# Router logits of a gated decoder stack: the two parts of the router's weights side by side, and each half's logits in one block ahead of the next units' first products

## The reference

```python
logits = tokens @ router_w.T                 # 1024 tokens x 8 experts
topv, topi = jax.lax.top_k(logits, K)        # K = 2
w = jax.nn.softmax(topv, axis=-1)
gate = jnp.zeros((T, n_experts)).at[jnp.arange(T)[:, None], topi].add(w)
for e in range(n_experts):
    h = jax.nn.gelu(tokens @ w1[e].T, approximate=False)
    out = out + gate[:, e:e + 1] * (h @ w2[e].T)
```

## Time and profile before

| | |
|---|---|
| median of 3 runs | 146.15 us (144.23, 146.15, 146.25) |
| the profiled execution | span 144.6 us from first to last instruction, 1996 instructions; no other time is given for it |
| TensorE, its weight loads | busy 121.0 us (84%), 86.0 us (59%) |
| VectorE | busy 116.2 us (80%) |
| ScalarE, GpSimd | busy 79.8 us (55%), 37.4 us (26%) |
| chain that ended last | TensorE 50%, VectorE 26%, issue 10%, ScalarE 6%, DMA 4% |

### The profile page before, as it was taken

The page is one execution under the profiler, slowest core; times in us unless marked ns, Lnnn a source line. Parts: engine busy times, 40 slices in busy tenths (PEclk is TensorE's granted clock), DMA queues, the critical chain, the costliest instruction groups (busy, mean ns, idle before and its releaser), DMA issues.

```text
span 144.6 us, 1996 instructions
## 1 busy us (share of the span) xinstructions
PE 121.0 (84%) x622; PEld 86.0 (59%) x622; DVE 116.2 (80%) x325; ACT 79.8 (55%) x149; POOL 37.4 (26%) x58
## 2 busy tenths in 40 slices
PE   6999999999999999999999968999999700049890
PEld 4787768486656567876555847777758500035570
DVE  5888985997329999999496986888398899899873
ACT  3343495745565576975453242173438899880540
POOL 1009302310569400396003704422010003000000
PEclk9999999999999999999999977999999995556998
DMA  4996000002079522320000000000000000000004
GB/s 130 300 410 239 0 0 0 0 0 65 24 221 345 159 73 75 97 99 22 5 0 0 0 2 0 0 5 2 0 0 0 0 0 2 0 5 0 0 0 145
DMA packets 4413, 8.76 MB, mean 61 GB/s; under 512 B 417, under 2 KB 1825, under 8 KB 4146
## 3 DMA queue, kind: packets, MB, share of 16 engines
q1 hardware_dynamic: 4400, 8.62, 17.4%
q10 hardware_dynamic: 2, 0.00, 0.0%
HBM read 8.07 MB, written 0.56 MB: 60 GB/s over the span
## 4 chain that ended last, share of the span: by engine, by line
PE 50%; DVE 26%; issue 10%; ACT 6%; DMA 4%; POOL 2%; DVEq 0%; POOLq 0%
PE bank L1378 5%; PE bank L1211 4%; PE bank L1330 4%; PE bank L1335 4%; PE bank L1364 4%; PE bank L1332 4%; DVE hidden L940 3%; PE bank L1238 3%; DVE amax_g L1103 3%; PE bank L1218 3%; PE bank L1483 3%; DMA q_exp<-gates 3%; DVE amax_p L1112 2%; PE bank L1235 2%; PE bank L1537 2%
## 5 line engine op out<-in xcount | busy, mean ns | idle before, releaser
L1211 PE MATMUL bank<-zero 128*128 128x256 f16 x159 | 24.5, 305 | 15.7 <-ACT ng L669 13.7
L1211 PEld LDWEIGHTS bank<-zero 128*128 128x128 f16 x159 | 16.8, 109 | 20.2 <-ACT ng L669 14.2
L544 ACT ACTIVATE hidden<-bank 128x512 f32<-128x512 f32 x32 | 18.5, 592 | 11.9 <-PE bank L1335 10.6
L1330 PE MATMUL bank<-xhi,we_hi 128*128 128x512 f32 x32 | 17.3, 540 | 0.0
L940 DVE TENSOR_TENSOR hidden<-hidden,q_exp 128x512 f32<-128x512 f32 x12 | 9.8, 838 | 5.4 <-DMA q_exp<-gates 3.5
L1332 PE MATMUL bank<-xhi,we_lo 128*128 128x512 f32 x32 | 12.7, 396 | 0.0
L1335 PE MATMUL bank<-xlo,we_hi 128*128 128x512 f32 x32 | 12.6, 405 | 0.0
L1378 PE MATMUL bank<-hidden,wexp 128*128 128x512 f32 x24 | 12.0, 595 | 0.0
L413 POOL TENSOR_TENSOR we_lo<-wexp,we_hi 128x256 fp32r<-128x256 f32 (+1 forms) x8 | 7.5, 950 | 12.7 <-DVE gate L875 9.9
L550 ACT ACTIVATE high_parts<-hidden 128x512 fp32r<-128x512 f32 x12 | 7.6, 634 | 5.2 <-DVE hidden L940 5.1
L400 POOL TENSOR_TENSOR rstd<-var,neg_half 128x4 f32<-128x4 f32 x7 | 7.1, 1019 | 12.9 <-DVE var L717 12.8
(11 more groups left out here) (261 smaller groups left out, 291.8 us busy)
## 6 DMA issues: line engine op xcount, KB each, us to landing
wexp<-in_experts SPq DMA_DIRECT2D x2, 1024.0 KB, 8.5
q_exp<-gates SPq DMA_DIRECT2D x6, 256.0 KB, 3.5
q_soft<-gates SPq DMA_DIRECT2D x6, 256.0 KB, 3.5
wq<-in_lpbq SPq DMA_DIRECT2D x1, 576.0 KB, 10.5
stream<-in_x SPq DMA_DIRECT2D x2, 256.0 KB, 4.0
xn<-gates SPq DMA_DIRECT2D x1, 512.0 KB, 5.9
x<-gates SPq DMA_DIRECT2D x1, 512.0 KB, 6.7
pa<-in_packa SPq DMA_DIRECT2D x1, 325.0 KB, 3.2
```

The costliest lines, as they stand in the source:

```text
L544: act.activation(ge[p % NB][:, :], bank[4 + p % NB][:, :], ACT.Gelu).then_inc(gelu_done, 1)
L1211: mm(bank[b][:, 0:256], zero16[:, 0:128], zero16[:, 0:256], start=True, stop=True)
L1330: mm(out_, w_hi[e][:, k], half(xhi, h), start=True, stop=False)
```

## The change

The router's two weight parts now lie side by side in one tile `rw_both` of 16 columns. Each tile of tokens takes two products in place of three: high tokens by all 16 columns, and low tokens by the first 8, added to the first 8 columns of the result. A tile's result is 16 wide in PSUM, and VectorE adds the two groups of eight with a reduction that takes the place of the copy. The eight products of a half now stand in one block, and the first products of the two units that stood between them follow as a `first_pair`.

```diff
-        rw_hi = sb("rw_hi", [128, EXPERTS], f32r)
-        rw_lo = sb("rw_lo", [128, EXPERTS], f32r)
+        rw_both = sb("rw_both", [128, 2 * EXPERTS], f32r)
+        rw_hi, rw_lo = (rw_both[:, k * EXPERTS:(k + 1) * EXPERTS] for k in range(2))
...
-                dve.tensor_copy(lg, bank[2 + h][:, 0:TILES * EXPERTS].rearrange("p (t e) -> p t e", e=EXPERTS))\
+                dve.tensor_reduce(lg, bank[2 + h][:, 0:TILES * 2 * EXPERTS].rearrange(
+                    "p (t k e) -> p t e k", k=2, e=EXPERTS), X, ALU.add)\
                     .then_inc(lg_read, 1)
...
-            def logits(h, beside):
+            def logits(h):
                 pe.wait_ge(xlo_ready, h + 1)
                 for t in range(TILES):
                     k = slice(h * HT + t * D, h * HT + (t + 1) * D)
-                    at = t * EXPERTS
-                    last = three(bank[2 + h][:, at:at + EXPERTS], xhi[:, k], xlo[:, k], rw_hi[:, :], rw_lo[:, :],
-                                 True, True)
-                    if t < TILES - 1:
-                        z_passes(beside[t // 2], (0, 1) if t % 2 == 0 else (2,))
+                    at = t * 2 * EXPERTS
+                    mm(bank[2 + h][:, at:at + 2 * EXPERTS], xhi[:, k], rw_both[:, :], start=True, stop=False)
+                    last = mm(bank[2 + h][:, at:at + EXPERTS], xlo[:, k], rw_hi, start=False, stop=True)
                 last.then_inc(lg_mm, 1)
-                z_passes(beside[1], (2,))
...
-            logits(0, (2, 3))
+            logits(0)
+            first_pair(2)
             y_first(0)
...
             first_pair(4)
-            logits(1, (6, 7))
+            logits(1)
+            first_pair(6)
             y_first(4)
```

More of the change, by code:

```diff
@@ L901, in _ @@
             rstd_of(1)
-            link(dve.tensor_copy(rw_hi[:, :], A("rwT", EXPERTS)))
-            dve.tensor_tensor(rw_lo[:, :], A("rwT", EXPERTS), rw_hi[:, :].bitcast(f32), ALU.subtract)\
+            link(dve.tensor_copy(rw_hi, A("rwT", EXPERTS)))
+            dve.tensor_tensor(rw_lo, A("rwT", EXPERTS), rw_hi.bitcast(f32), ALU.subtract)\
                 .then_inc(rw_ready, 1)
```

## The result

The changed kernel takes 144.37 us (median of 20 runs, 143.45 to 144.93), the kernel before 145.26 us (20 runs, 144.11 to 146.25): ratio 0.994, 95% interval 0.9913 to 0.9967. It is 0.9 us faster; 0.76 was forecast. The median of before is lower than in the three runs that the prediction had, and the measured 144.37 lies in its range of 143.5 to 146.5, but not in its narrower 145.0 to 145.8: of the 1.03 us between 145.4 and 144.37, 0.89 are the three runs' high start of 146.15. The median of before is a weak number also with 20 runs: their times lie in two groups of ten, 144.11 to 145.09 and 145.44 to 146.25, and 145.26 is the middle of the gap. The profiled execution's own time is 143.45 us with a span of 141.7 us.

What follows compares the result with a forecast made beforehand. It took the chain through TensorE, then half 1's gates, write and broadcast, into a units' stage without slack as the bound. Terms 0.38 + 0.42 - 0.04 = 0.76 us off 146.15 gave 145.4 us, range 143.5 to 146.5.

Steps and rivals of the forecast that it cites:

- The price of a small product: TensorE's router products: 0.11 us each from start to start, eight making 0.90 us; grouping the others neither costs nor saves.
- Term 1: Half 0: four fewer products bring y products 0.44 us earlier; 0.38 us passes through ScalarE to half 1's tokens.
- The first rival: ScalarE's late GELUs get through no faster, so term 1 does not arrive: 0.38 us gain, 145.8 us; chance 0.12.
- Term 2: Half 1, VectorE: its wait for the logits goes, 0.42 of 0.46 us gained.
- Term 3: Half 1, VectorE: the 64-element reduction replacing the 0.19 us copy takes 0.23, losing 0.04 us (0 to 0.22).
- The sum: Gates of half 1: 0.38 + 0.42 - 0.04 = 0.76 us earlier, giving 145.4 us.
- the stage behind the broadcast passes it on one for one: Units' stage: TensorE, VectorE and ScalarE all enter about 0.76 us earlier, so it ends 0.76 earlier.
- nothing in that stage has slack: Units' stage behind the broadcast: engines work in step; TensorE and VectorE both busy 4.00 of 4 us from 56 to 60.
- The second rival: Behind the gates: a broadcast landing as late as before, or the unit loop's own bound, returns the gain; 146.15 us, chance 0.08.
- the fourth rival: TensorE's low clock near 86 us costs 1.15 us on eight products; missed 144.2 us, more met 146.5; chance 0.14 either way.
- the weights' work in VectorE's queue: Half 1, VectorE: of 1.9 us by which TensorE has the logits ready earlier, this work covers 1.1 us.
- under 2% can't be told from none: Whole kernel: a change under 2% either way is about what measurement cannot tell from none; chance of within 2% 0.92.

Runs made afterwards that it cites:

- the gates first: Changed kernel, plus half 1's logits read before the weights' scales and rounding, gates transposed before unit 8, copied before expert 0's output; ratio to the kernel before 0.9916.
- the block alone: Kernel before, still three products a tile and the copy, but all twelve of a half in one block, the units' passes behind as a pair; ratio 0.9988.
- the repeats: No edit: changed kernel again (ratio 0.9957 to the kernel before), then both kernels profiled once more; first unit pass to first keys-and-values product 56.48 us before, 55.58 changed.
- the transposes between the y products: The gates first, plus TensorE's wait for VectorE's attention reads moved behind half 0's logits and gate transposes between units 4 and 5's y products; ratio to before 0.9892.

## Why the prediction was right

- **The price of a small product** (0.11, grouping neutral) was right: 0.88 for eight (the prediction's sum had 0.90), 1.34 for twelve, and the four removed save 0.45 in each half (0.44, and 0.37 to 0.45, were forecast).
- **Term 1** was 0.38 and measured 0.41 to 0.43: the high tokens' copy moved from 7.00 to 6.58 on the yardstick, VectorE's low tokens from 7.62 to 7.21. The step that was a little off is ScalarE's start behind the late GELUs. They began where forecast (4.12 on the yardstick), but half 1's normalisation moved by 0.23 us in place of 0.17, so that 0.43 of TensorE's 0.44 reached the copy of expert 0's output (6.50 to 6.07). The first rival (term 1 lost) is out.
- **Term 2** was mis-sized: 0.42 forecast, 0.54 measured; from low tokens to the read it takes 5.32 in place of 5.86. I had let the read begin at the listed end of the rounding, 33.04; it began 0.08 before that listed end (at 31.60, against 30.32 + 1.36 = 31.68), and the 0.04 that I had laid between them was not there either.
- **Term 3** was 0.04 and measured 0.03: the reduction takes 0.22 us, the copy took 0.19. The Trainium skill's warning in "VectorE: DVE Perf Modes", section "Rules for kernel authors", that a reduction is the engine's slowest operation, is no obstacle at 64 elements. The difference is the 0.03 us that follows from the formula in that page's section on the trn2 errata (an estimated 0.19 against 0.16), though both instructions take 0.03 longer than it gives.
- **The sum** of 0.76 was 0.92 at the gates (15.67 to 14.75) and 0.89 at their copy. I had summed along VectorE's gates, but what moves the copy is TensorE's coming to the transposes, which it does without a wait before and after, 0.90 us earlier (16.04 to 15.14) where I had 0.75 to 0.83. Terms 2 and 3 count only as far as they keep VectorE's gates ahead of that: from the gates to the copy it takes 1.00 us before and 1.03 after, and 0.97 where TensorE waits for them, so they are ahead by hundredths. Both ways gave nearly the same number; that is why the sum held. At the end of the experts 0.90 arrived. That the stage behind the broadcast passes it on one for one was right: 34.4 to 34.6 us in all kernels whose gates are copied no earlier than 15.4. That nothing in that stage has slack was read from the one stretch of 56 to 60 us and is too strong: from 38 to 76 us TensorE's weight loads waited 3.3 us for VectorE's low parts in the kernel before, and the gates first gained 0.13 us. The second rival is out, with its own reason partly right: the broadcast's landing does vary, by 0.50 us between two executions of before and by 0.40 among three of the changed kernel.
- **The clock** is the fourth rival and happened in the profile, not in the medians: one of three profiles of the changed kernel misses the low stretch around 85 us, and neither of the two of before does. For the other runs only the mean granted clock of the execution is on record; in the profiles it is 0.947 or 0.952 where the stretch is missed and 0.935 to 0.937 where it is met. A mean of 0.947 or more stands beside 22 of 58 runs of before and 13 of 32 of the changed kernel, so the runs show no change in how often it is missed. Open is why the gain differs with it: on one chip the medians are 144.40 and 144.10 at a mean clock of 0.947 or more, and 145.93 and 144.93 below. No profile shows the kernel before at the higher mean clock, so what differs there is not known; the yardstick itself ends at 73.9 to 76.9 us, ahead of the low stretch.

That the weights' work in VectorE's queue covers 1.1 us of the earlier logits, as the prediction had it, was shown by putting the gates first (the read at 11.42 in place of 12.53). That the copy goes by TensorE's place was not in its sum, and the block alone showed it. And that under 2% can't be told from none was too careful: the interval of 20 runs of each kernel leaves out 1.

## What to carry to other kernels

Small products of one tile each cost 0.11 us here, with 8 columns or 16, in a block or spread. Their weight loads start at the same distance (20.81, 20.92, 21.03), so I take those for the price, which no run tested by itself. Putting two sets of columns side by side behind one load removes products, while grouping them only brings their result forward, and that is worth what its reader's queue and the next step's place in the other queues let through. Measure a change of under 1% between two events inside the profile that both kernels share: at the gates' copy they repeat to 0.01 us and at the end of the experts, behind the transfer, to 0.4, where the two spans differ by another 1.9 us that the repeats don't show again. Before a gain is counted through a chain, look at each engine's place in it: VectorE's queue held half 1's gates by 1.1 us and TensorE's by another 0.4 (from the gates built to their copy 1.42 us with the gates first, 0.97 with the transposes between the y products), and each had to be taken away in its own queue.

## What the runs showed of the hardware

The same write and broadcast (16 KB out, 256 KB back) took from ScalarE's copy to the waiting engine between 5.20 and 5.85 us in eleven executions. In the execution with 5.85 SyncE needed 1.95 us to issue the two broadcasts that followed, in the others 0.91. The granted clock fell to 0.50 near 85 us in one execution of a kernel and not in another of the same kernel, and cost 1.15 us on eight products. In five executions VectorE's read of half 1's logits, which waited for nothing, started 0.08 to 0.09 us before the listed end of the rounding ahead of it, so a queue's length is read from starts, not from ends. Near 85 us the low clock costs the part behind the experts about 1 us: 66.68 to 66.70 us in three executions without it, 67.65 to 67.96 in eight with it.
